# Normalising the dense diffusion of a four-layer graph network through TensorE

## The reference

```python
h = jnp.maximum(_layernorm(x, axis=-1), 0.0)        # (x - mean) / sqrt(var + 1e-5)
h = h @ W.T + b                                     # W is 64x64
agg = segment_sum(norm[:, None] * h[col], row)      # edges and self loops
out = h + 0.05 * (agg - h) + 1.5 * relu(h)
x = x + out
```

## Time and profile before

| | |
|---|---|
| median of three runs | 6699.57 us (6690.15 to 6706.76) |
| the profiled execution | 6710.78 us, its span 6709.1 us |
| mean granted TensorE clock | 0.847 |
| busy over the span | PE 4395.3 us, DVE 4366.9 us, POOL 3785.6 us, ACT 1838.5 us |
| dense diffusion, first load issued to last GpSimd product | 256.3 to 652.0 us |

### The profile page before, as it was taken

One profiled execution on the slowest core, in us unless ns is written; L12 is line 12 of the kernel. 1 busy time (PEld: TensorE's weight loads), 2 busy tenths in 40 slices (PEclk: granted clock), 3 DMA queues, 4 the chain that ended last, 5 costly groups with the idle time before them and its releaser, 6 DMA issues. The chain is left out here.

```text
span 6709.1 us, 96894 instructions
## 1 busy us (share of the span) xinstructions
PE 4395.3 (66%) x29117; PEld 3843.5 (57%) x29194; DVE 4366.9 (65%) x5674; ACT 1838.5 (27%) x2782; POOL 3785.6 (56%) x3348
## 2 busy tenths in 40 slices
PE   6665445771078878566565877766787856865887
PEld 3454344661067777555555865555787745755775
DVE  7898544224667778778798852224988955862458
ACT  5543112330033444333333421111453410000001
POOL 0398665773077757577763767774000047757756
PEclk9766667996589999877778988889998978988999
DMA  6398766677955558433334864544678851231109
GB/s 239 93 276 264 160 143 145 142 142 257 394 174 167 174 177 260 149 99 95 98 105 135 272 185 139 144 138 131 211 254 298 309 192 42 58 123 14 14 17 300
DMA packets 865593, 1128.43 MB, mean 168 GB/s; under 512 B 591583, under 2 KB 604276, under 8 KB 864060
## 3 DMA queue, kind: packets, MB, share of 16 engines
q1 hardware_dynamic: 409660, 807.13, 35.8%
q10 hardware_dynamic: 311296, 226.11, 11.1%
q0 software_dynamic: 144256, 90.12, 9.3%
HBM read 633.88 MB, written 495.44 MB: 168 GB/s over the span
## 5 line engine op out<-in xcount | busy, mean ns | idle before, releaser
L897 POOL DMA_INDIRECT gc_msgs<-t,src_rows x784 | 753.6, 961 | 1112.9 <-POOLq L148 816.2
L2080 PE MATMUL gc_ring<-gc_msgs,gc_hot 128*128 x4736 | 650.9, 296 | 239.0 <-SPq L2039 233.7
L2080 PEld LDWEIGHTS gc_ring<-gc_msgs,gc_hot 128*128 128x128 f32 x4736 | 624.2, 209 | 310.5 <-issue 303.1
L951 POOL DMA_INDIRECT acc<-de_sums,de_put x392 | 607.6, 1550 | 303.8 <-issue 149.8
L897 POOL DMA_INDIRECT edge_rows<-h,dst_rows x392 | 379.7, 969 | 231.7 <-issue 116.5
L897 POOL DMA_INDIRECT at1s_ends<-x,src_rows x392 | 409.8, 1045 | 168.7 <-issue 117.4
L897 POOL DMA_INDIRECT edge_rows<-x,dst_rows x392 | 387.7, 989 | 166.4 <-issue 117.4
L897 POOL DMA_INDIRECT re_rows<-x,src_rows x392 | 405.9, 1035 | 125.4 <-issue 125.1
L897 POOL DMA_INDIRECT at2s_ends<-h,src_rows x392 | 370.8, 946 | 142.4 <-issue 119.0
L1503 PE MATMUL re_psR<-w_rel,re_own 128*128 128x128 f32 x3136 | 396.2, 292 | 71.7 <-DVE re_own L1440 71.3
L1503 PEld LDWEIGHTS re_psR<-w_rel,re_own 128*128 128x128 f32 x3136 | 388.9, 207 | 80.5 <-issue 77.8
(11 more groups left out here) (539 smaller groups left out, 11250.2 us busy)
## 6 DMA issues: line engine op xcount, KB each, us to landing
rew_win<-x SPq DMA_DIRECT2D x74, 544.0 KB
at1w_win<-g SPq DMA_DIRECT2D x74, 544.0 KB
at2w_win<-g SPq DMA_DIRECT2D x74, 544.0 KB, 4.1
de_win<-t ACTq DMA_DIRECT2D x74, 512.0 KB, 4.5
de_near<-same SPq DMA_DIRECT2D x74, 512.0 KB, 5.0
x<-rew_win SPq DMA_DIRECT2D x74, 512.0 KB
h<-at1w_win SPq DMA_DIRECT2D x74, 512.0 KB
h<-at2w_win SPq DMA_DIRECT2D x74, 512.0 KB, 2.9
```

The costliest lines, as they stand in the source:

```text
L897: nc.gpsimd.indirect_dma_start(buf[:, t * width:(t + 1) * width], None, table, bass.IndirectOffsetOnAxis(ap=rows[:, t:t + 1], axis=0)).the ...
L951: nc.gpsimd.indirect_dma_start(g.acc0[j % LANES], bass.IndirectOffsetOnAxis(ap=put[:, j:j + 1], axis=0), sums[:, j * D:(j + 1) * D], None, ...
L2080: done = nc.tensor.matmul(ring[:, bass.ds(to[n], SLOT)], hot[k][:, n, :], each_group(msgs[:, bass.ds(of[n], MID)], SLOT // MID), start=Fal ...
```

## The change

VectorE no longer centres, sums or scales the input. TensorE turns the raw x (8 transposes into psT); ScalarE copies it out (xT). TensorE multiplies by `off_mean`, the identity less 1/64 in each 64x64 half, in two products with 512 moving columns, into psC: that is the centred, turned tile. ScalarE reads psC twice, with a relu to hT and a square to sqT. TensorE then sums the squares with 8 products against `each_half` (two columns) into psV, and multiplies hT by w0 into psH. ScalarE takes the root of psV, VectorE scales the projected rows psH by its reciprocal, adds the bias (now read from PSUM), and makes the reaction as 2.45 * max(h * 0.95/2.45, h), in one instruction for the maximum (`steeper`) and one for the blend. GpSimd keeps two products; its addition and ScalarE's second relu are gone. psT, psC and psH have one buffer each. `mean_off` remains for other stages. `times`, `transpose_pairs`, `once_past` and `held` are unchanged.

```diff
--- before.py
+++ after.py
@@ -755,19 +755,20 @@
 
     W = J * D
     with Room(nc, g, "dd") as r:
-        x, cen, lo, hi = ([r.sb(f"{n}{k}", [P, W]) for k in range(DEEP)] for n in ("x", "cen", "t0", "base"))
-        sq, hT, h0, rl = ([r.sb(f"{n}{k}", [P, W]) for k in range(2)] for n in ("sq", "hT", "h0", "rl"))
+        x, lo, hi = ([r.sb(f"{n}{k}", [P, W]) for k in range(DEEP)] for n in ("x", "t0", "base"))
+        xT, sqT, hT, h0 = ([r.sb(f"{n}{k}", [P, W]) for k in range(2)] for n in ("xT", "sqT", "hT", "h0"))
+        steeper = r.sb("steeper", [P, W])
         sd = r.sb("sd", [P, DEEP, J])
-        few = r.ps("few", [P, 2 * DEEP, J])
-        sums, inverse = few[:, 0:DEEP, :], few[:, DEEP:2 * DEEP, :]
-        psT = r.ps("psT", [P, W])
-        psH = [r.ps(f"psH{k}", [P, W]) for k in range(2)]
+        off_mean, each_half = r.sb("off_mean", [P, P]), r.sb("each_half", [P, 2])
+        psT, psC, psH = (r.ps(n, [P, W]) for n in ("psT", "psC", "psH"))
+        psV, bias = r.ps("psV", [P, 512]), r.ps("bias", [P, 512])
         x_in = [r.sem(f"x_in{k}") for k in range(DEEP)]
         stored = [r.sem(f"stored{k}") for k in range(DEEP)]
         last_in = r.sem("last_in")
         grow = r.sb("grow", [P, COLS])
-        x_free, o_free, link_s, squared, centred, summed, rooted, normed, turned, evac, product, h_made, mixed, relued, scaled, ready, cleared, lo_made, blended = (r.sem(n) for n in (
-            "x_free", "o_free", "link", "squared", "centred", "summed", "rooted", "normed", "turned", "evac", "product", "h_made", "mixed", "relued", "scaled", "ready", "cleared", "lo_made", "blended"))
+        x_free, o_free, link_s, laid, turned, copied, centred, squared, product, rooted, read, h_made, lo_made, blended, ready, cleared = (r.sem(n) for n in (
+            "x_free", "o_free", "link", "laid", "turned", "copied", "centred", "squared", "product", "rooted", "read", "h_made", "lo_made", "blended", "ready", "cleared"))
+        UP = 2.45
         with nc.Block() as block:
             @block.sync
             def _(sp):
@@ -790,61 +791,55 @@
 
             @block.vector
             def _(dve):
+                v = nc.vector
                 link = Link(dve, link_s)
 
-                def centre(b):
-                    s = b.slot
+                def close(b):
+                    s = b.slot
+                    h = h0[s % 2]
                     link.restart()
-                    dve.wait_ge(x_in[s], 16 * b.nth)
-                    mean_off(nc, link, x[s][:, :], cen[s][:, :], sums[:, s, :], J).then_inc(centred, 1)
-
-                def variance(b):
-                    s = b.slot
-                    dve.wait_ge(squared, b.number + 1)
-                    nc.vector.tensor_reduce(sd[:, s, :], grouped(sq[s % 2][:, :], D), AXX, ALU.add).then_inc(summed, 1)
-
-                def scale(b):
-                    s = b.slot
                     dve.wait_ge(rooted, b.number + 1)
-                    link(nc.vector.reciprocal(inverse[:, s, :], sd[:, s, :]))
-                    nc.vector.tensor_tensor(grouped(cen[s][:, :], D), grouped(cen[s][:, :], D), spread(inverse[:, s, :], D), ALU.mult).then_inc(normed, 1)
-
-                def close(b):
-                    s = b.slot
-                    dve.wait_ge(product, b.number + 1)
-                    dve.wait_ge(scaled, b.number + 1)
+                    link(v.reciprocal(sd[:, s, :], sd[:, s, :]))
+                    once_past(dve, lo_made, b, 2)
+                    v.tensor_tensor(grouped(h[:, :], D), grouped(psH[:, :], D), spread(sd[:, s, :], D), ALU.mult).then_inc(read, 1)
+                    dve.wait_ge(read, b.number + 1)
                     dve.wait_ge(o_free, b.number + 1)
-                    nc.vector.tensor_tensor(grouped(h0[s % 2][:, :], D), grouped(psH[s % 2][:, :], D), each_group(g.w["b0"][:, :], J), ALU.add).then_inc(h_made, 1)
+                    v.tensor_tensor(grouped(h[:, :], D), grouped(h[:, :], D), each_group(bias[:, 0:D], J), ALU.add).then_inc(h_made, 1)
                     dve.wait_ge(h_made, b.number + 1)
-                    nc.vector.scalar_tensor_tensor(hi[s][:, :], h0[s % 2][:, :], 0.95, x[s][:, :], ALU.mult, ALU.add).then_inc(blended, 1)
-
-                link(nc.vector.reciprocal(grow[:, :], g.dis[:, :]))
-                link(nc.vector.tensor_scalar(grow[:, :], grow[:, :], 20.0, None, ALU.mult))
-                pipeline(dve, order=[(2, scale), (1, variance), (3, close), (0, centre)], slots=DEEP)
+                    link(v.scalar_tensor_tensor(steeper[:, :], h[:, :], 0.95 / UP, h[:, :], ALU.mult, ALU.max))
+                    v.scalar_tensor_tensor(hi[s][:, :], steeper[:, :], UP, x[s][:, :], ALU.mult, ALU.add).then_inc(blended, 1)
+
+                link(v.memset(off_mean[:, :], 0.0))
+                v.memset(off_mean[0:D, 0:D], -1.0 / D)
+                link(v.memset(off_mean[D:P, D:P], -1.0 / D))
+                link(v.tensor_tensor(off_mean[:, :], off_mean[:, :], g.ident[:, :], ALU.add))
+                link(v.memset(each_half[:, :], 0.0))
+                v.memset(each_half[0:D, 0:1], 1.0)
+                link(v.memset(each_half[D:P, 1:2], 1.0))
+                v.tensor_copy(bias[:, 0:D], g.w["b0"][:, :]).then_inc(laid, 1)
+                dve.wait_ge(laid, 1)
+                link(v.reciprocal(grow[:, :], g.dis[:, :]))
+                v.tensor_scalar(grow[:, :], grow[:, :], 20.0, None, ALU.mult).then_inc(laid, 1)
+                pipeline(dve, order=[(2, close)], slots=DEEP)
 
             @block.scalar
             def _(act):
-                def norm(b):
-                    s = b.slot
+                def root(b):
+                    s = b.slot
+                    act.wait_ge(product, b.number + 1)
+                    nc.scalar.activation(sd[:, s, :], psV[:, 0:J], ACT.Sqrt, bias=g.eps[:, :], scale=1.0 / D).then_inc(rooted, 1)
+
+                def square(b):
+                    s = b.slot % 2
                     act.wait_ge(centred, b.number + 1)
-                    if not (isinstance(b.number, int) and b.number < 2):
-                        act.wait_ge(summed, b.number - 1)
-                    nc.scalar.activation(sq[s % 2][:, :], cen[s][:, :], ACT.Square).then_inc(squared, 1)
-
-                def root(b):
-                    s = b.slot
-                    act.wait_ge(summed, b.number + 1)
-                    nc.scalar.activation(sd[:, s, :], sd[:, s, :], ACT.Sqrt, bias=g.eps[:, :], scale=1.0 / D).then_inc(rooted, 1)
-
-                def turn(b):
-                    s = b.slot
+                    once_past(act, product, b, 2)
+                    nc.scalar.activation(hT[s][:, :], psC[:, :], ACT.Relu)
+                    nc.scalar.activation(sqT[s][:, :], psC[:, :], ACT.Square).then_inc(squared, 1)
+
+                def copy(b):
                     act.wait_ge(turned, b.number + 1)
-                    nc.scalar.activation(hT[s % 2][:, :], psT[:, :], ACT.Relu).then_inc(evac, 1)
-
-                def positive(b):
-                    act.wait_ge(h_made, b.number + 1)
-                    once_past(act, mixed, b, 2)
-                    nc.scalar.activation(rl[b.slot % 2][:, :], h0[b.slot % 2][:, :], ACT.Relu, scale=1.5).then_inc(relued, 1)
+                    once_past(act, centred, b, 2)
+                    nc.scalar.activation(xT[b.slot % 2][:, :], psT[:, :], ACT.Copy).then_inc(copied, 1)
 
                 def store(b):
                     s = b.slot
@@ -857,22 +852,38 @@
                     act.wait_ge(stored[b.slot], 48 * b.nth)
                     act.sem_inc(o_free, 1)
                 act.sem_inc(o_free, DEEP)
-                pipeline(act, order=[(1, norm), (1, root), (2, turn), (3, positive), (5, store), (6, landed)], slots=DEEP)
+                pipeline(act, order=[(2, root), (1, square), (0, copy), (4, store), (6, landed)], slots=DEEP)
 
             @block.tensor
             def _(pe):
+                def multiply(b):
+                    s = b.slot % 2
+                    pe.wait_ge(squared, b.number + 1)
+                    once_past(pe, rooted, b, 1)
+                    for j in range(J // 2):
+                        nc.tensor.matmul(psV[:, 2 * j:2 * j + 2], sqT[s][:, j * P:(j + 1) * P], each_half[:, :], start=True, stop=True)
+                    once_past(pe, read, b, 1)
+                    times(nc, psH, hT[s], g.w["w0"], J // 2).then_inc(product, 1)
+
+                def centre(b):
+                    s = b.slot % 2
+                    pe.wait_ge(copied, b.number + 1)
+                    once_past(pe, squared, b, 1)
+                    for h in range(2):
+                        last = nc.tensor.matmul(psC[:, h * 512:(h + 1) * 512], off_mean[:, :], xT[s][:, h * 512:(h + 1) * 512], start=True, stop=True)
+                    last.then_inc(centred, 1)
+
                 def turn(b):
                     s = b.slot
-                    pe.wait_ge(normed, b.number + 1)
-                    transpose_pairs(nc, psT, cen[s], g.ident, J // 2).then_inc(turned, 1)
```

(62 more changed lines are left out.)

## The result

The changed kernel took 6740.5 us (median of five runs, 6735.4 to 6742.4) against 6703.7 us for the kernel before (five runs, 6690.2 to 6708.1): 37 us slower, a ratio of 1.0055 with a 95% interval of 1.0044 to 1.0065. The forecast was 6706 us and no change. The time lies inside the range on record (6674 to 6752), but on the slower side of the 0.3% bound, where rival B (the clock) stood with a chance of 0.22. The profiled execution took 6735.4 us, its span 6733.7.

A forecast was written before the change was run, and what follows sets the result against it. VectorE bounds the kernel before; afterwards a TensorE-ScalarE loop of 7.67 us, 7.84 with the clock, over 48 steps from 274 us, plus 8.9, ends at 659.2 instead of 652.0: +7.2 us on the median, written as 6706 us, range 6674 to 6752.

The forecast's parts named there:

- rival B: Dense diffusion: TensorE's granted clock stays under 0.93; 6738 us at 0.87, 6765 at 0.80, 6830 at 0.67; chance 0.22.
- What bounds the kernel before: Dense diffusion before the change: VectorE, busy 49.1 of 50 us, sets the 7.63 us step; transfers merely stretch.
- The loop that sets the pace: Changed stage: TensorE products and centring, then ScalarE relu and square, in turn; 7.67 us a step at full clock.
- I take 0.97: 5.55 x (1/0.97 - 1) = 0.17 us more, 7.84 us a step: Clock of the changed stage, slowing TensorE's 5.55 us of the loop; 0.97 resembles the skip stage's 0.93 to 0.97.
- The start: Beginning of the changed stage: the first step's products start at about 274 us (272 to 276).
- the tail: End of the stage, from the last step's products at 650.3 to GpSimd's last product at 659.2: 8.9 us.
- VectorE and GpSimd: Changed stage: VectorE about 5.6 us a step, GpSimd 5.9; even blocking each other, VectorE's 7.8 adds nothing to 7.84.
- the 2 us of VectorE: Changed stage: VectorE work freed per step, over 2 us, if nothing else is slower.
- the alternating case: VectorE and GpSimd blocking each other in turn on SBUF reads: VectorE at 6.6 us a step, not deciding.
- The two-column products: TensorE's sums of squares: the weight load sets the cost, so two columns cost 1.84 us, like 64 or 128.
- Rival D: Two-column cost follows the columns: loop 6.0 us, result 6680 or 6646 us; chance 0.13 for faster by over 0.3%.

The follow-up runs named there:

- e6: Kernel before with only the reaction as a VectorE maximum, without ScalarE's second relu and GpSimd's addition: 6813 us, 1.0179 to the kernel before.
- e5: Changed kernel with TensorE order centre, turn, multiply, ScalarE order square, copy, root, and GpSimd's first product behind the blend: 6623 us, 0.9901 to the kernel before.
- e9: Changed kernel with four idle products in TensorE's gap and 64 instead of 2 moving columns in the sums of squares: 0.9998 to the kernel before.
- e2: Changed kernel with ScalarE squaring first and relu second, each with its own signal: 6652 us, 0.9940 to the kernel before.
- e3: Changed kernel with TensorE order centre, turn, multiply and ScalarE order square, copy, root, store: 6656 us, 0.9929 to the kernel before.
- e1: Changed kernel with four idle products in TensorE's gap behind each tile's transposes: 1.0049 to the kernel before.
- e7: Changed kernel with 64 instead of 2 moving columns in the sums of squares, 62 of them zeros: 1.0046 to the kernel before.
- e4: Changed kernel with GpSimd's first product waiting for VectorE's blend: 1.0044 to the kernel before.

## Why the prediction was right and wrong

**What bounds the kernel before: right.** VectorE, by e6. The transfers are elastic: e5 moved 342 GB/s at a share of 1.08 where the earlier trace rows shows 275 at 0.96.

**The loop that sets the pace: right.** Forecast 1.84 + 1.84 + 1.87 + 1.92 + 0.2 = 7.67 us at the full clock; measured 7.58 to 7.67 in the short rounds and in all rounds of e9, 7.61 on average. The terms: two-column products 1.80, products 1.87, centring 1.72, from there to the next round 2.19. e2 took one activation out of the loop and the round fell by 0.91 us; e3 took both out and TensorE's wait for ScalarE was gone.

**The clock: wrong, and nearly all of the miss.** The step "I take 0.97: 5.55 x (1/0.97 - 1) = 0.17 us more, 7.84 us a step" failed twice. First, the value. From product(0) to product(48) the clock was 0.90, not 0.97:

```profile
275.30:679.40 404.10, 346.64 (x2105) 274.03 (x2103) 322.96 (x240) 149.29 (x191) 223.73 (x96) 0.90 0.71 235
```

The forecast had taken 0.97 from the skip stage, because that has one gap of the same length in a step. e1 shows that the gap alone is not what counts: with it filled, nothing changed. Second, the formula was wrong in form. It spreads the low stretches evenly over a step, where they fell into the products and the centring, all on the path. Then each microsecond at the lower level costs half a microsecond of the round, and the cost is a step times (1 - clock): 8.42 x 0.10 = 0.84 us, near the measured 8.42 - 7.61 = 0.81, while the formula at 0.90 gives 0.62. In the sum, the clock's value makes 0.45 us a step (0.62 - 0.17) and the form 0.19 (0.81 - 0.62), and the loop itself was 0.06 shorter than forecast: 0.58 us a step too little (8.42 - 7.84), times 48, 28 us. The start gave 1.3 us (275.3 for 274) and the tail 0.5 (9.4 for 8.9). Together 29.6 us, from 659.2 to 688.8. Rival B had named the direction, but with the same formula, which gives about 6728 us at 0.90. Its 6738 goes with a clock of 0.87, which was not measured, so that it lies near 6740 is luck.

**What makes the clock fall: partly settled.** In the steady part of the stage the falls that the rows show lie in the product group or at its edge, behind transposes, gap and two-column products. Filling the gap alone (e1) leaves 21 long rounds and filling the columns alone (e7) 20, where the changed kernel has 22; both together (e9) leave none and hold the clock at 1.00. So neither was enough and both together were; why is not shown. The length of the gap is not the measure: e2 and e1 leave nearly the same one (0.28 and 0.32 us a step), and e2 has four long rounds, e1 21. How much of it the transposes make was not separated. Nor is it explained why e3, with 6.17 us of work and waits of about 0.5 us or less, had long rounds in its first half (six, of 8.2 to 8.6 us) and e5, in the same order, none.

**VectorE and GpSimd: right in effect, rough in size.** VectorE needed 6.7 us a step, not 5.6: the blend is held up in every step, by 1.6 us. So the change did not free the 2 us of VectorE that the forecast counted on, but 0.8: it was busy for 7.5 us of a step before and 6.7 after (5.2 in e4). The bounds had this between 5.4 and 7.8, the alternating case at 6.6. By the rule of the Trainium skill ("SBUF — State Buffer", the section with the single rule on the shared port pair) the instruction that starts first keeps the port for its whole length and the other waits. The trace agrees: maximum 1.22, then GpSimd's product, which spans 2.76 us where it takes 1.90 alone, then the blend, 2.81. e4 undid both by order alone. Neither was on the path, as forecast.

**The two-column products: right.** Rival D, that their cost follows the columns, is refuted by 1.80 us for 2 columns beside 1.84 for 64. The group's 16 weight loads fill it:

```profile
422.42 1.86 PEld L864 LDWEIGHTS dd_psV<-dd_each_half,dd_sqT 128*128 128x128 f32 x16 [1.40 <-ACT dd_sqT L837]
```

The estimate of 1.7 us from the load time of the Trainium skill ("TensorE: Matmul & The Clock Gate", section on LDWEIGHTS) was close. The floor of about 25 ns from that page of the Trainium skill, in its section on the back-to-back gap, does not bind here: a record takes 112 ns.

## What to carry to other kernels

When the bound engine is relieved, write down the loop of waits between the other engines before counting the gain. Here the work taken off VectorE was worth nothing (0.8 us a step, or 2.3 with GpSimd one wait later) as long as ScalarE's two activations stood between two TensorE groups with one buffer, and an order in which other groups run beside them, with one wait moved on GpSimd, made the stage's work cheap enough that the whole ran 1% faster than the kernel before. Price low clock by a step times (1 - clock) if the low stretches can fall on the path, at nothing where another engine is the bound (e3), and don't borrow a clock from a stage because its gap looks alike: look at what TensorE does around the gap too. Where VectorE and GpSimd both read SBUF, the hold-up follows the order of their instructions, and one more VectorE instruction can cost twice its length.

## What was not expected of the hardware

- The granted clock stayed at 0.91 with TensorE busy for 97% of 300 us (e1), and rose to 1.00 at 96% with other columns (e9).
- The alternation was regular: rounds of 7.6 and 9.3 us nearly in turn, in four kernels (the changed one, e1, e4, e7).
- A product group with 2 moving columns takes 1.80 us for 16 records, one with 64 columns 1.84; its weight loads are busy for 1.86.
- The DMA share read 0.97 at 275 GB/s and 1.08 at 342 GB/s with the same transfers, so a share near 1 was no bound.
- VectorE's blend took 2.81 us in each of 49 steps, 1.22 in each of 49 with GpSimd one wait later.
